# Two-layer attention and feed-forward kernel: order and form of the first layer's shared expert, and a wait count on each pair of row gathers

## The reference

```python
var = jnp.mean(jnp.square(hidden_states), axis=-1, keepdims=True)
normed = hidden_states * jax.lax.rsqrt(var + 1e-08) * norm_weight
shared = jnp.maximum(normed @ sw1 + sb1, 0.0) @ sw2 + sb2          # 128 -> 512 -> 128, every token
flat = normed.reshape(-1, d)
probs = jax.nn.sigmoid(flat @ router_w.T)
scores, idx = jax.lax.top_k(probs, TOPK)                           # 2 of 8 experts
w = scores / (jnp.sum(scores, axis=-1, keepdims=True) + 1e-06)
comb = comb.at[jnp.arange(T)[:, None], idx].add(w)
h = jnp.maximum(jnp.einsum('td,edh->teh', flat, ew1) + eb1[None, :, :], 0.0)
eo = jnp.einsum('teh,eho->teo', h, ew2) + eb2[None, :, :]
routed = jnp.einsum('teo,te->to', eo, comb)
return shared + routed.reshape(b, s, -1)
```

## Time and profile before

| | us |
|---|---|
| median of 3 runs | 884.38 (883.95 to 891.09) |
| the profiled execution | 888.71 |
| its span on the core | 886.9 |
| shared-expert stage | 213 to 341 |
| block loop | 341 to 598 |

### The profile page before, as it was taken

How to read it: one execution, slowest core, us unless ns; L and a number is a source line. 1 busy time by engine, 2 the same in 40 slices (tenths; PEclk the granted TensorE clock), 3 DMA queues, 4 the chain that set the end, 5 groups by cost and what they waited for, 6 DMA issues and landing times. The chain is left out here.

```text
span 886.9 us, 19516 instructions
## 1 busy us (share of the span) xinstructions
PE 729.6 (82%) x6628; PEld 540.6 (61%) x6654; DVE 541.9 (61%) x1395; ACT 510.1 (58%) x824; POOL 315.9 (36%) x495
## 2 busy tenths in 40 slices
PE   6899999995738775599995189998488899998997
PEld 5556666663626653488884078887255566665453
DVE  6788887673646672255551046656387798776563
ACT  4468888883615761255552045555267688886343
POOL 5755554213378547200006700002666533112110
PEclk9989999997668886699997589998689899999699
DMA  6686554611012221012112111205855434410011
GB/s 201 101 173 122 114 104 102 132 32 50 25 55 83 78 84 54 30 49 72 46 49 62 53 49 48 58 25 143 130 108 102 109 74 78 79 38 2 13 37 47
DMA packets 72369, 66.76 MB, mean 75 GB/s; under 512 B 8114, under 2 KB 63316, under 8 KB 72020
## 3 DMA queue, kind: packets, MB, share of 16 engines
q1 hardware_dynamic: 57764, 51.88, 26.5%
q0 software_dynamic: 4096, 8.40, 3.4%
q10 hardware_dynamic: 10416, 5.25, 2.1%
HBM read 21.55 MB, written 16.65 MB: 43 GB/s over the span
## 5 line engine op out<-in xcount | busy, mean ns | idle before, releaser
L576 DVE TENSOR_REDUCE a_negmax<-psum 128x4 f32<-128x512 f32 x256 | 164.6, 685 | 8.6 <-PE psum L690 7.2
L443 ACT ACTIVATE temp<-psum 128x1024 f32<-128x1024 f32 x128 | 131.1, 1024 | 22.1 <-PE psum L708 16.2
L1323 DVE TENSOR_TENSOR f_h_lo<-psum,f_h_hi 128x512 fp32r<-128x512 f32 x78 | 53.9, 692 | 108.2 <-ACT f_h_hi L1106 95.1
L690 PE MATMUL psum<-a_k_stack,a_q_stack 96*128 96x256 bf16 x512 | 84.2, 282 | 7.5 <-DVE a_negmax L576 6.1
L722 PE MATMUL psum<-temp,a_v_st 128*18 128x128 f32 x2048 | 81.8, 277 | 5.2 <-ACT temp L443 1.6
L971 POOL DMA_INDIRECT xs<-scratch,slots x64 | 67.9, 1061 | 48.0 <-DVE slots L1240 30.0
L1099 ACT ACTIVATE f_hid<-psum 128x512 f32<-128x512 f32 x78 | 46.6, 597 | 61.6 <-PE psum L1450 40.7
L708 PE MATMUL psum<-a_q_stack,a_k_stack 128*128 128x128 bf16 x1024 | 80.0, 222 | 1.2 <-ACT temp L443 0.5
L708 PEld LDWEIGHTS psum<-a_q_stack,a_k_stack 128*128 128x128 bf16 x1024 | 65.3, 100 | 17.0 <-issue 16.1
L722 PEld LDWEIGHTS psum<-temp,a_v_st 128*18 128x18 f32 x2048 | 46.6, 97 | 47.4 <-issue 39.4
L377 POOL CAST a_nm_cols<-a_negmax 128x16 bf16<-128x16 f32 x64 | 13.6, 212 | 172.7 <-DVE a_negmax L576 172.6
(11 more groups left out here) (231 smaller groups left out, 1672.8 us busy)
## 6 DMA issues: line engine op xcount, KB each, us to landing
a_k_stack<-a_k_parts SPq DMA_DIRECT2D x192, 64.0 KB
a_q_stack<-a_q_parts SPq DMA_DIRECT2D x96, 128.0 KB
xs<-zeros ACTq DMA_DIRECT2D x8, 640.0 KB, 5.1
f_w_in<-in_f_w SPq DMA_DIRECT2D x18, 256.0 KB
scratch<-xs SPq DMA_DIRECT2D x18, 256.0 KB, 3.4
ys<-f_hid SPq DMA_DIRECT2D x18, 256.0 KB, 2.4
scratch<-in_ctx SPq DMA_DIRECT2D x16, 256.0 KB
x<-in_x SPq DMA_DIRECT2D x8, 256.0 KB, 5.5
```

The source lines that it names most:

```text
L443: nc.scalar.activation(pt[:, unit].rearrange("p a b t -> p (a b t)"), ps[:, bank:bank + 2].rearrange("p a n -> p (a n)"), ACT.Exp, scale=S ...
L576: nc.vector.tensor_reduce(negmax[:, b % 2, :, 2 * unit:2 * unit + 2].rearrange("p n b -> p b n"), ps[:, P1_BANK + unit % 2].rearrange("p ( ...
L690: last = nc.tensor.matmul(ps[:, P1_BANK + unit % 2, 2 * j * P:2 * (j + 1) * P], q_cols(b, blk, STACK_ROWS), k_cols(b, blk, STACK_ROWS, sli ...
L1323: nc.vector.tensor_tensor(h_lo[:, n % 2], ps[:, H_BANKS[n % 2]], h_hi[:, n % 2], ALU.subtract,).then_inc(s["bh_lo"], 1)
```

## The change

In the shared-expert stage:

- The bias of the first layer goes into PSUM as one more product (`s_rows`, three bf16 parts, against ones), 32 products of 512 columns in all. `relu` is gone; `high` is now the ReLU out of PSUM itself, and `low` on DVE reads PSUM and does max and subtraction in one operation. The semaphore `relu` is gone too; a quarter's PSUM bank is free when its `low` is done.
- `up` and `down` go by quarters. PE's list alternates `down(g, hb)` and `up(g + 1, hb)`, with `transpose_out`, `transposes` and `logits` between the quarters.
- `low(0)` stands ahead of `route(0)` and `low(1)` ahead of `places(0)` on DVE; `low(7)` stands ahead of `route(1)`. `statistics(4)` moves behind `places(0)`, `split_biases` to the front.
- `warm()`: 10 idle products of 128 columns, 4 times at the stage's start and once in each of three gaps after it (70 in all).
- On POOL two memsets of `b1_rows` and `b2_rows` move from the start of the stage behind `x_low(3)`, `scales(4)` moves ahead of the first scatter, and the other `scales` and `x_low` come a little earlier among the scatters.

In the block loop each pair of gathers waits for a count of finished blocks, and the adds move to match:

```diff
@@ POOL @@
                     for b in range(HALF):
+                        pool.wait_ge(s["by"], HBLK + 3 + 3 * b // 2)
                         for n in range(2):
                             pool.indirect_dma_start(yg[n][:, b], None, self.ys[0:HBLK * P],
@@ DVE @@
-                    ADD_AT = [HBLK + 14 + 3 * b // 2 for b in range(HALF)]
+                    ADD_AT = [HBLK + 14 + 6 * (b // GB) + b % GB for b in range(HALF)]
```

The core of the rest:

```diff
@@ POOL @@
+                    nc.gpsimd.memset(b1_rows[:], 0.0).then_inc(s["rows_zero"], 1)
+                    nc.gpsimd.memset(b2_rows[:], 0.0).then_inc(s["rows_zero"], 1)
+
+                    scales(G // 2)
                     pool.wait_ge(self.cleared_rows, 16 * G)
                     pool.wait_ge(s["xn"], G // 2)
                     for b in range(HALF):
                         scatter(b)
-                        g = G // 2 + (b - 2) // 3
+                        g = G // 2 + 1 + (b - 2) // 3
                         if (b - 2) % 3 == 0 and b >= 2 and g < G:
                             scales(g)
-                        g = G // 2 + (b - 6) // 3
-                        if (b - 6) % 3 == 0 and b >= 6 and g < G:
+                        g = G // 2 + (b - 4) // 3
+                        if (b - 4) % 3 == 0 and b >= 4 and g < G:
                             x_low(g)
@@ ACT @@
-                        nc.scalar.activation(h_hi[:, hb], hid[:, hb], ACT.Copy).then_inc(s["h_hi"], 1)
+                        nc.scalar.activation(h_hi[:, hb], ps[:, UP_BANK + hb], ACT.Relu).then_inc(s["h_hi"], 1)
@@ DVE @@
+                    def low(g, hb):
+                        dve.wait_ge(s["h_hi"], HB * g + hb + 1)
+                        wait(dve, s["down"], HB * (g - 1) + hb + 1)
+                        nc.vector.scalar_tensor_tensor(h_lo[:, hb], ps[:, UP_BANK + hb], 0.0, h_hi[:, hb].bitcast(F32),
+                                                       ALU.max, ALU.subtract).then_inc(s["h_lo"], 1)
...
+                    for hb in range(HB):
+                        low(0, hb)
                     route(0)
+                    for hb in range(HB):
+                        low(1, hb)
+                    places(0)
                     statistics(4)
-                    places(0)
                     block_experts(0)
                     for g in range(G):
-                        lows(g)
-                        split_weights(g + 1)
+                        if g > 0:
+                            accumulate(g - 1)
+                        split_weights(g + 1, 0)
                         if g < G // 2:
                             norm(4 + g)
+                        if g + 2 < G:
+                            low(g + 2, 0)
+                            low(g + 2, 1)
+                        split_weights(g + 1, 1)
+                        if g + 2 < G:
+                            low(g + 2, 2)
+                            low(g + 2, 3)
+                        if g < 3:
+                            statistics(5 + g)
+                        if g == 5:
                             route(1)
-                        if g == 5:
+                        if g == 6:
                             places(1)
@@ PE @@
+                    warm()
+                    transposes(3)
+                    up(0, 0)
+                    up(0, 1)
+                    logits(2)
+                    logits(3)
+                    up(0, 2)
+                    up(0, 3)
                     for g in range(G):
...
+                        for hb in range(HB):
+                            if hb == 0 and g == 0:
+                                pe.wait_ge(s["xT"], G // 2)
+                            down(g, hb)
+                            if g + 1 < G:
+                                up(g + 1, hb)
+                            if hb == 0 and g > 0:
+                                transpose_out(g - 1)
+                            if hb == 1 and 0 < g <= G // 2:
+                                transposes(G // 2 + g - 1)
+                            if hb == 1 and 1 < g <= G // 2 + 1:
+                                logits(G // 2 + g - 2)
+                        if g == 0:
+                            prefix(0)
+                        if g == G // 2 + 2:
+                            prefix(1)
```

More of the change, by code:

```diff
@@ L905, in _ @@
                     for n, e in enumerate(order):
+                        if n == 2:
+                            sp.wait_ge(s["b_low"], 1)
+                            for part in range(3):
+                                sp.dma_start(s_rows[part:part + 1], b_parts[E0 * HB:NE * HB, part]).then_inc(s["s_rows"], 16)
                         if n >= 2:
@@ L1250, in block_experts @@
                         nc.vector.tensor_copy(block_of[:, HSLOT * h:HSLOT * (h + 1)], blockf[:]).then_inc(s["block_of"], 1)
-                    def lows(g):
-                        for hb in range(HB):
-                            dve.wait_ge(s["h_hi"], HB * g + hb + 1)
-                            wait(dve, s["down"], HB * (g - 1) + hb + 1)
-                            nc.vector.tensor_tensor(h_lo[:, hb], hid[:, hb], h_hi[:, hb], ALU.subtract,
-                                                    ).then_inc(s["h_lo"], 1)
+                    def low(g, hb):
[3 more added lines that the diff above has]
+                                                       ALU.max, ALU.subtract).then_inc(s["h_lo"], 1)
                     def accumulate(g):
@@ L1266, in _ @@
                     statistics(1)
+                    split_biases()
                     for g in range(G // 2):
@@ L1290, in _ @@
                             gates()
-                        if g > 1:
-                            accumulate(g - 2)
-                    accumulate(G - 2)
                     accumulate(G - 1)
@@ L1396, in prefix, with warm @@
                                          ).then_inc(s["prefix"], 1)
+                    def warm():
+                        for n in range(WARM):
+                            nc.tensor.matmul(ps[:, UP_BANK + 3, bass.ts(n % GB, P)], self.ident16[:], self.ident16[:],
+                                             start=True, stop=True)
+                    for _ in range(4):
+                        warm()
                     pe.wait_ge(s["small_in"], 64)
@@ L1402, in _ @@
                     transposes(0)
-                    for g in range(G // 2):
-                        if g + 1 < G // 2:
-                            transposes(g + 1)
-                        logits(g)
-                    up(0)
-                    up(1)
-                    prefix(0)
-                    pe.wait_ge(s["xT"], G // 2)
-                    for g in range(G):
-                        if G // 2 < g + 4 <= G:
-                            logits(g + 3)
-                        if g == 5:
-                            prefix(1)
-                        down(g)
-                        if g > 0:
-                            transpose_out(g - 1)
-                        if g < G // 2:
-                            transposes(G // 2 + g)
-                        if g + 2 < G:
-                            up(g + 2)
+                    warm()
+                    transposes(1)
+                    logits(0)
+                    warm()
+                    transposes(2)
+                    logits(1)
+                    warm()
+                    transposes(3)
[5 more added lines that the diff above has]
+                    up(0, 3)
+                    for g in range(G):
+                        for hb in range(HB):
+                            if hb == 0 and g == 0:
+                                pe.wait_ge(s["xT"], G // 2)
+                            down(g, hb)
+                            if g + 1 < G:
+                                up(g + 1, hb)
[8 more added lines that the diff above has]
+                        if g == G // 2 + 2:
+                            prefix(1)
                     transpose_out(G - 1)
```

104 lines of the change are left out of this document (50 added, 54 removed).

## The result

| | before | after |
|---|---|---|
| median of 4 runs | 887.05 (883.95 to 891.09) | 861.79 (853.85 to 865.44) |
| ratio, 95% interval | | 0.970 (0.962 to 0.978) |
| the profiled execution, its span | 888.71, 886.9 | 853.85, 852.1 |

The account below looks back on a forecast made before the run. No engine is full; the block loop stalls because PE's signals are late while POOL issues indirect DMAs without a pause. 888.7 + 1 - 2.5 - 16.1 = 871.1, about 867 us as a median, range 845 to 890.

Parts of the forecast that it names:

- my own case: Block loop's gathers: a paced pair costs 0.83 to 2 us, giving 858 to 876 us; chance 0.40.
- ACT's first late pass: Sign in the profile after: it comes right as the block loop starts, near 324.
- The reading of the two stalls: Block loop, 341 to 366 and 470 to 513: PE's signals are late while POOL issues indirect DMAs without a pause.
- The paced gathers: Block loop: 38.5 us lost at the gathers go, 22.4 us for 16 paced pairs come, -16.1 us.
- I take 1.4, since it is the same loop: Block loop's gathers: cost of a lone pair, taken from the first lateness; 16 x 1.4 = 22.4 us.
- rival 1: Block loop's gathers: pacing is nearly free, 0.83 us a pair or less, 844 to 858 us; chance 0.27.
- The shared stage: First scatter starts at 251.9 to 256.4, 4.5 to 9 us later; end of the second half's scatters +1 us.
- The loop's earlier start: Block loop starts 17 us sooner, near 324, with scatters under it; one block gained, -2.5 us (0 to -7.5).
- the two terms: Later end of the second half's scatters, +1 us, and one block gained by the loop's sooner start, -2.5 us.
- Rival 2: Block loop: the loss doesn't come from the gathers' rate; same late signals stay, 880 to 888 us; chance 0.14.
- Rival 3: Block loop's gathers: each pair costs more than in the burst, deciding from 3 us a pair, up to 919; chance 0.11.
- Rival 4: Shared stage: the cold chain puts the second half's scatters 9 us later, 875 to 877 us; chance 0.08.

Follow-up runs that it names:

- b_paced_gathers: The kernel before with only the wait on each pair of gathers and the adds' new turns; 855.56 us, ratio 0.966.
- a_paced_scatters: The changed kernel with the second half's scatters, after the first two pairs, also paced at one pair in 1.5 blocks; 837.70 us, ratio 0.944.
- o_plain_pool: The changed kernel without waits on the gathers, each gather replaced by a plain copy of 128 rows issued by POOL; one run, 858.09 us.
- o_compute: The changed kernel without waits on the gathers, each gather replaced by a POOL subtraction of about 1 us; one run, 848.19 us.
- b_rates: The kernel before with second-half scatters paced one pair per block and gathers one pair in two blocks; 839.41 us, ratio 0.950.
- b_singles: The kernel before with gathers and second-half scatters paced, every single indirect DMA waiting for one more block; 827.88 us, ratio 0.936.
- a_old_gathers: The changed kernel without the waits on the gathers and with the adds at their old turns; 890.96 us, ratio 1.006.
- p_no_warm: `a_paced_scatters` without the 70 idle products of the shared stage; 831.92 us, ratio 0.941.
- o_fixed_expert: The changed kernel without waits on the gathers, block k taking expert k modulo 8, so PE loads no register per block; one run, 889.27 us.
- after_again: The changed kernel run once more, unaltered, for its spread and a second trace; 864.17 us, ratio 0.967.

## Why the prediction came out right

I predicted 867 us with 845 to 890; it is 861.8. The direction, the place and most marks in the profile held, but two terms of the sum were off, and they partly cancelled: that the time lies 5 us from my number, and inside my own case's 858 to 876, is in part luck. One mark failed. ACT's first late pass was to come right as the loop starts; it waited for a product that was over by 337.9, 8 us after the start.

**The reading of the two stalls** held. Both go with indirect DMAs issued without a pause, and both shrink to some 6 us when those are spread (`b_paced_gathers`, `a_paced_scatters`). I had written that I see the pattern and not its cause; `o_plain_pool` and `o_compute` narrow it to the DMAs with row indices.

**The paced gathers, -16.1, were mis-sized: -32.1.** The step that failed is "I take 1.4, since it is the same loop". 1.4 us was how late the first signal came, not what the loop lost by it. Nor was it the effect of one pair: when ACT took that signal up at 473.01, POOL was issuing the second pair:

```profile
471.25 0.94 POOL L1012 DMA_INDIRECT f_x_hi<-ys,slots  x1 [0.30 <-issue]
472.50 0.94 POOL L1012 DMA_INDIRECT f_x_lo<-ys,slots  x1 [0.30 <-issue]
```

The trace after shows a block 2.3 us late and the next two 1.22 and 1.84 us apart, so that 16 pairs cost 6.6 us, 0.41 each, below the 0.83 that I had as the nearest row from below. `b_rates` and `b_singles` show that the price isn't one of a pair at all, but of the rate. So at the gathers rival 1 came true, not my case: its condition was 0.83 us a pair or less, and its 844 to 858 holds `b_paced_gathers` with 855.6. The changed kernel lies above that range because the new stage costs time.

**The shared stage, 4.5 to 9 us on the first scatter, was too small.** In absolute times it seemed to hold: the first scatter at 253.99 (252 to 256 forecast), the second half's slots at 324.3 (319 to 328), their last scatter at 364.67 (360 to 370). But this run's first attention ended early. Against the transposed group it is +9.6 us in this run and +12.7 in `a_old_gathers`. The time between the starts of route and slots was nearly well sized (239.46 to 250.93, 11.5 us, where I had 10.3 to 10.8; `route(0)` itself I took as 3.9 us, while the earlier trace rows give 4.3):

```profile
239.46 0.28 DVE L1158 TENSOR_REDUCE f_top<-f_prob 128x16 f32<-128x128 f32 x1
...
247.09 0.41 DVE L1202 TENSOR_TENSOR_SCAN attn_w<-psum,zero 128x128 f32<-128x128 f32 x1
...
250.93 0.18 DVE L1243 CAST slots<-f_slotf 128x32 uint32<-128x32 f32 x1
```

The failed step is the start of `route(0)`: 13.1 us after `copy_xT(0)` before (235.06 - 222.0), 20.5 in this profile (239.46 - 219.0) and 23.2 in `a_old_gathers` (245.25 - 222.1), 7 to 10 us later and not 4 to 8. From the first scatter to the second half's slots it took 70.3 us, inside the 67 to 72.

**The loop's earlier start, -2.5.** The start was to be near 324 and came at 329.6. In the profile the start and the first 36 blocks together give -1.4 us, near the -1.5 of the two terms. By medians (`a_old_gathers`) the new stage costs 0.2 to 0.9%, some 2 to 8 us. I had 17.6 us of gain, 16.1 from the gathers and 1.5 from the stage. By medians the 25 us measured are 30 from the gathers (`b_paced_gathers`: 887.0 times 0.034) less about 5 from the stage. The intervals of the ratios are wide enough that this split is good to some 4 us only.

**Rival 2** (the loss isn't from the gathers' rate) is out. I had drawn it from the Trainium skill's SBUF page (SBUF — State Buffer, "SBUF: two separate sides"). By that rule the traffic is innocent, and in that the runs agree: `o_plain_pool` moves the same bytes at a higher rate and loses 0.8 us. What failed is what I made of it. No compute operation was slowed (ACT's passes take 0.60 us in the stalls as elsewhere); what came late was the signal from one engine to the next, and a rule on traffic says nothing of that. **Rival 3** (3 us a pair) is out with 0.4. **Rival 4** (the scatters slip by 9) happened in part (the second half's slots 8 to 13 us later behind the first transposed group); I take it for the 5 us above.

**The idle products.** The clock did rise (0.60 to 0.79 in 213 to 248, where real products were added too). `p_no_warm` shows that the idle ones raise it for a few us, and no time for it.

## What stays open

Why PE's signals are late in the block loop and not in the shared stage. In the kernel before, the second half's scatters run without a rest from 320 on, and the shared stage's last products fall in their midst. PE's last product of one `up` quarter and ACT's pass on it, and 15 us further on PE's transposes and DVE's sum:

```profile
323.59 0.63 PE L1362 MATMUL psum<-f_x_lo,f_ws_hi 128*128 128x512 f32 x1
...
338.23 0.60 PE L1386 MATMUL psum<-ident,temp 128*128 128x128 f32 x4
```

```profile
324.26 0.69 ACT L1037 ACTIVATE f_hid<-psum,f_b 128x512 f32<-128x512 f32 x1 [0.53 <-PE psum L1362]
```

```profile
338.86 0.69 DVE L1261 TENSOR_TENSOR x<-psum,x 128x512 f32<-128x512 f32 x1 [4.15 <-issue]
```

Product over by 324.22, taken up at 324.26; transposes over by 338.83, taken up at 338.86, 19 us into the scatters. Five microseconds later, with the same scatters going on, the last product of block 0's `up` is over, and it is taken up 4.7 us late. The register load and computed addresses are excluded but for 2 to 3 us (`o_fixed_expert`), POOL's load and its queue's traffic too. The shape of the products, their number between two signals, or how many engines wait for them weren't tried. Nor was the second attention, where the gathers of the second half still run as pairs.

That it is the signal which is late, and not the product, is argued and not shown: the ends of products are modelled in these profiles. For it speaks that the last products of `block_down` that DVE took up only at 367.03 had begun by 347.79 and PE, which runs its list in order, had begun the next transpose behind them at 348.68.

## What to carry to other kernels

When several engines sit idle at once and none of their operations is longer, compare when a producer's instruction ends with when its consumer starts: a gap there is news that came late, and what goes on elsewhere in just those stretches is the suspect. Spread indirect DMAs over the loop they run under, by a wait on the loop's own count; one to a block of 2.48 us cost nothing here. And price a disturbance by what the loop has lost some blocks later, not by how late the first event is.

## What the runs showed of the hardware

- While POOL issues indirect DMAs back to back (0.95 us each, 0.3 us between), what PE has done in this block loop is taken up late by ACT and DVE: by 1.7 us, then 4.8, then 18 to 20 us in the first stall after (the last of these 1.4 to 3.5 us after POOL stops), by 4.7 us at the start of the first stall before. What ACT and DVE have done is taken up on time (within 0.1 us). With one indirect DMA in 2.48 us the loop keeps its pace.
- The shared stage, under the same scatters, isn't held up: PE's transposes are taken up 0.03 us after they end, 19 us into the burst.
- Plain DMAs issued by POOL on the same queue, 0.55 us each without a pause, and 39.6 us of POOL arithmetic without a pause, hardly delay the loop (0.8 and 0.3 us lost).
- The first attention, with the same code in all kernels, ended at 211.2, 218.0 and 220.0 us in `after`, `a_paced_scatters` and `after_again`, with a granted clock of 1.00, 0.94 and 0.90 in 50 to 100.
